# A transformer layer on one core: VectorE's order in the prologue, the first step's tables of units, and the place of the last Tanh

## What is computed

```python
qkv = einsum('bse,fe->bsf', layernorm(x), in_proj_weight) + in_proj_bias
scores = where(blocked, -inf, einsum('bhqd,bhkd->bhqk', q * scale, k))
x = x + einsum('bse,fe->bsf', softmax(scores) @ v, out_proj_weight) + out_proj_bias
h = layernorm(x) @ weight @ aux_weight1 @ aux_weight2
x = x + tanh(h + bias)
```

## Time and profile before

| | us |
|---|---|
| median of 3 runs | 1992.54 |
| lowest and highest | 1991.99 and 1997.41 |
| the profiled execution's own time | 1995.04 |
| its span | 1993.3 |
| ACT busy in it | 1911.1 (96%) |
| PE busy in it | 1819.7 (91%) |
| DVE, POOL busy in it | 1005.1, 440.7 |

### The profile page before, as it was taken

How to read it: one execution, slowest core, us unless ns; L and a number is a source line. 1 busy time by engine, 2 the same in 40 slices (tenths; PEclk the granted TensorE clock), 3 DMA queues, 4 the chain that set the end, 5 groups by cost and what they waited for, 6 DMA issues and landing times.

```text
span 1993.3 us, 101806 instructions
## 1 busy us (share of the span) xinstructions
PE 1819.7 (91%) x47112; PEld 750.0 (38%) x47112; DVE 1005.1 (50%) x1723; ACT 1911.1 (96%) x2099; POOL 440.7 (22%) x458
## 2 busy tenths in 40 slices
PE   6899999999999999999999999999998889888895
PEld 3443343343434434343343434334343323223232
DVE  5333346556474564747556474655635333342432
ACT  4699999999999999999999999999999999999993
POOL 2000004132050412305141130504113210313001
PEclk9999999999999999999999999999999999999998
DMA  4410111101221111111212111111022111000001
GB/s 135 119 51 25 46 33 49 41 28 40 80 76 47 44 38 33 49 36 54 59 53 69 38 51 36 49 49 33 19 78 56 33 32 30 27 22 29 25 25 45
DMA packets 95523, 93.89 MB, mean 47 GB/s; under 512 B 19626, under 2 KB 86634, under 8 KB 95090
## 3 DMA queue, kind: packets, MB, share of 16 engines
q1 hardware_dynamic: 94580, 86.86, 14.8%
q10 hardware_dynamic: 512, 0.47, 0.1%
HBM read 52.56 MB, written 25.72 MB: 39 GB/s over the span
## 4 chain that ended last, share of the span: by engine, by line
ACT 60%; issue 31%; PE 6%; DVE 1%; DMA 1%; POOL 0%; ACTq 0%; SPq 0%; DVEq 0%; POOLq 0%
ACT probs L1362 60%; PE outs L1431 2%; PE scores L1410 1%; PE ps_qk L510 1%; PE spare L1459 0%; PE scores L1628 0%; PE spare L1518 0%; DVE xn L382 0%; DMA inverse<-row_inverse 0%; DVE stats L371 0%; PE ps_turn L483 0%; POOL rstd L314 0%; DMA xin<-in_x 0%; PE spare L1446 0%; PE scores L1646 0%
## 5 line engine op out<-in xcount | busy, mean ns | idle before, releaser
L1362 ACT ACTIVATE probs<-scores 128x1024 f32<-128x1024 f32 x2048 | 1881.1, 1113 | 20.4 <-PE scores L1410 19.9
L1431 PE MATMUL outs<-probs,vs 64*32 64x512 f32 x16384 | 1073.9, 590 | 0.9 <-ACT probs L1362 0.6
L1410 PE MATMUL scores<-qs,ks 49*32 49x512 f16 x16384 | 834.6, 382 | 130.5 <-ACT probs L1362 127.1
L1410 PEld LDWEIGHTS scores<-qs,ks 49*32 49x32 f16 x16384 | 231.6, 89 | 1055.1 <-ACT probs L1362 1032.1
L1431 PEld LDWEIGHTS outs<-probs,vs 64*32 64x32 f32 x16384 | 301.0, 106 | 27.8 <-issue 5.5
L967 DVE TENSOR_TENSOR probs<-probs,allowed 128x320 f32<-128x320 f32 (+2 forms) x280 | 157.0, 564 | 213.6 <-ACT probs L1362 212.1
L875 POOL TENSOR_TENSOR s_squares<-s_qk_f 128x512 bf16<-128x512 f32 x48 | 61.6, 1282 | 293.7 <-DVE s_qk_f L1037 293.7
L1470 PE MATMUL spare<-s_xt,w_qkv 64*32 64x256 f32 x3072 | 119.4, 376 | 0.0
L975 DVE COPY raw<-outs 128x512 f32<-128x512 f32 x32 | 22.1, 692 | 168.0 <-PE outs L1431 119.6
L919 POOL TENSOR_TENSOR t_over<-t_over,t_square 128x512 f32<-128x512 f32 x70 | 94.7, 1353 | 5.8
L861 POOL TENSOR_TENSOR s_var_eps<-s_mean_var,eps 128x4 f32<-128x4 f32 x12 | 2.4, 201 | 414.4 <-DVE s_mean_var L1008 414.4
(11 more groups left out here) (151 smaller groups left out, 1379.1 us busy)
## 6 DMA issues: line engine op xcount, KB each, us to landing
qs<-q_parts SPq DMA_DIRECT2D x192, 64.0 KB
ks<-k_parts SPq DMA_DIRECT2D x189, 64.0 KB
inverse<-row_inverse SPq DMA_DIRECT2D x32, 256.0 KB
shared<-in_x SPq DMA_DIRECT2D x64, 128.0 KB, 2.3
out<-s_pre SPq DMA_DIRECT2D x64, 128.0 KB, 1.9
ctx_in<-raw SPq DMA_DIRECT2D x248, 32.0 KB
s_xin<-in_x SPq DMA_DIRECT2D x48, 128.0 KB, 2.1
q_parts<-s_parts SPq DMA_DIRECT2D x24, 256.0 KB, 2.4
```

The source lines that it names most:

```text
L1362: act.activation(probs[:, u % RING, 2 * slot:2 * slot + 2].rearrange("p c q -> p (c q)"), scores[:, 2 * slot:2 * slot + 2].rearrange("p c ...
L1410: last = pe.matmul(scores[cols, 2 * slot + e], ks[rows, group, keys], qs[rows, group], start=True, stop=True)
L1431: last = pe.matmul(outs[32 * c:32 * c + 32, side], vs[keys, at:at + 2 * HD], probs[keys, u % RING, c], start=(i == 0), stop=(i == KBLOCKS ...
```

## The change

It has four parts.

1. **Prologue.** The first chunk of x comes as two DMAs of two tiles each, and VectorE's third bn_stats waits for the second. `xn_done` is raised for each tile of the first chunk, and TensorE transposes tile by tile (both halves of a tile, then the next). GpSimd's memset of `guard_row` waits for the four tiles and no longer for `rstd` alone. VectorE's order of a chunk becomes: normalise the next chunk first, two splits, `take_norms`, statistics of the chunk after next, two splits.
2. **First step.** Statistics and normalising of step 0 move from r = 0, 1, 5, 6 to r = 8, 9, 13, 14.
3. **Fold.** Each product becomes four pieces of `product` behind units 56 to 59 and 61, 62, 63, 66 (unit 66 is r = 2 of step 1), its sums in two PSUM banks; VectorE takes it with a copy and an add (`take_fold`) at units 60 and 67.
4. **Last Tanh.** It stands behind ScalarE's last Exp, and its addition on VectorE behind the last unit, ahead of `evacuate`.

```diff
-FOLD_AT = (56, 60)
+FOLD_AT = ((56, 57, 58, 59), (61, 62, 63, 66))
+NORMALISE_AT = (0, 1, 5, 6)
+FIRST_NORMALISE_AT = (8, 9, 13, 14)
-SQUASH_AT = {True: 73, False: 58}
...
-            sp.dma_start(xin[:, 0], x_tiles[0]).then_inc(x_in[0], 16)
+            sp.dma_start(xin[:, 0, 0:2], x_tiles[0][:, 0:2]).then_inc(x_in[0], 16)
+            sp.dma_start(xin[:, 0, 2:4], x_tiles[0][:, 2:4]).then_inc(x_rest_in, 16)
...
-            pool.wait_ge(rstd_done, 1)
+            pool.wait_ge(xn_done, TPC)
             pool.memset(guard_row[:], GUARD_K).then_inc(cleared, 1)
...
             def step(c):
                 par = c % 2
+                if c < CPB - 1:
+                    normalise_b(c + 1)
                 dve.wait_ge(parts_out[par], c // 2 * 64)
-                more = c < CPB - 1
-                if more:
-                    normalise_a(c + 1)
                 split(c, 0)
-                if more:
-                    normalise_b(c + 1)
                 split(c, 1)
                 if c:
                     take_norms(c - 1)
+                if c < CPB - 2:
+                    normalise_a(c + 2)
                 for j in range(2, 4):
                     split(c, j)
...
             normalise_b(0)
+            normalise_a(1)
...
-            pe.wait_ge(xn_done, 1)
-            turn(0, 0)
-            turn(0, 1)
+            for t in range(TPC):
+                pe.wait_ge(xn_done, t + 1)
+                for half in range(HALVES):
+                    first = pe.transpose(ps_turn[half][:, t * P:(t + 1) * P], xn[:, t, half * P:(half + 1) * P], ident[:])
+                    if t == TPC - 1:
+                        first.then_inc(turned, 1)
...
+            def take_fold(stage):
+                dve.wait_ge((a12_ready, ffn_ready)[stage], 1)
+                folded = (a12, keep["w_ffn"][:])[stage]
+                dve.tensor_copy(folded, spare[0][:].rearrange("p (h n) -> p h n", n=EMB)).then_inc(dve_step, 1)
+                dve.wait_ge(dve_step, next(dve_steps))
+                dve.tensor_tensor(folded, folded, spare[1][:].rearrange("p (h n) -> p h n", n=EMB), ALU.add
+                                  ).then_inc((a12_copied, ffn_copied)[stage], 1)
...
-                        if c == TAIL - 1 and at == SQUASH_AT[beside] + 2:
-                            add_squashed(c)
...
+            add_squashed(TAIL - 1)
             evacuate(f, 1)
...
-                for c, at, beside in finishing(step, r):
-                    if c == TAIL - 1 and at == SQUASH_AT[beside]:
-                        squash(c)
+            squash(TAIL - 1)
```

More of the change, by code:

```diff
@@ L370, in normalise_a @@
                 for t in range(TPC):
+                    if c == 0 and t == 2:
+                        dve.wait_ge(x_rest_in, 16)
                     dve.bn_stats(stats[:, t], xin[:, c, t]).then_inc(stats_step, 1)
@@ L383, in normalise_b @@
                                              ALU.subtract, ALU.mult)
-                last.then_inc(xn_done, 1)
+                    if c == 0:
+                        last.then_inc(xn_done, 1)
+                if c:
+                    last.then_inc(xn_done, 1)
             def split(c, j):
@@ L1257, in run_step @@
                             write_guard(step // CPB)
-                    if step == 0 and r == FOLD_AT[0] + 2:
-                        dve.wait_ge(a12_ready, 1)
-                        dve.tensor_copy(a12, spare[0][:].rearrange("p (h n) -> p h n", n=EMB)).then_inc(a12_copied, 1)
-                    if step == 0 and r == FOLD_AT[1] + 2:
-                        dve.wait_ge(ffn_ready, 1)
-                        dve.tensor_copy(keep["w_ffn"][:], spare[1][:].rearrange("p (h n) -> p h n", n=EMB)
-                                        ).then_inc(ffn_copied, 1)
+                    for stage in range(2):
+                        if step * STEP + r == FOLD_AT[stage][-1] + 1:
+                            take_fold(stage)
                     if finishes:
@@ L1433, in weigh @@
                 last.then_inc(summed, 1)
-            def fold_ffn(stage):
-                if stage == 0:
-                    pe.wait_ge(ffn_in, 3 * 16)
-                    pe.wait_ge(v_copied, (LATE + 1) * 2)
-                else:
-                    pe.wait_ge(a12_copied, 1)
-                left, right, done = ((a1t, a2s, a12_ready), (w1t, a12, ffn_ready))[stage]
-                for half in range(HALVES):
-                    for k in range(HALVES):
-                        last = pe.matmul(spare[stage][:, half * EMB:(half + 1) * EMB],
-                                         left[:, k, half * P:(half + 1) * P], right[:, k],
-                                         start=(k == 0), stop=(k == HALVES - 1))
-                last.then_inc(done, 1)
             def turned_tiles(tiles, pair, k):
@@ L1472, in product, with fold_ffn @@
                 return last
+            def fold_ffn(stage, i):
+                half, k = divmod(i, HALVES)
+                if i == 0:
+                    if stage == 0:
+                        pe.wait_ge(ffn_in, 3 * 16)
+                        pe.wait_ge(v_copied, (LATE + 1) * 2)
+                    else:
+                        pe.wait_ge(a12_copied, 1)
+                left, right, done = ((a1t, a2s, a12_ready), (w1t, a12, ffn_ready))[stage]
+                last = product(half * EMB, lambda rows, c: left[rows, k, half * P + 32 * c:half * P + 32 * c + 32],
+                               right[:, k], k)
+                if i == 3:
+                    last.then_inc(done, 1)
             def turn(step, i):
@@ L1607, in run_step @@
                             sum_squares(step)
-                    if step == 0 and r in FOLD_AT:
-                        fold_ffn(FOLD_AT.index(r))
+                    for stage in range(2):
+                        if u in FOLD_AT[stage]:
+                            fold_ffn(stage, FOLD_AT[stage].index(u))
                     for pair in range(2):
```

12 lines of the change are left out of this document (7 added, 5 removed).

## The result

| | before | after |
|---|---|---|
| median of the runs of this comparison, us | 1994.38 (4 runs) | 1979.57 (4 runs, 1977.76 to 1980.35) |
| ratio, 95% interval | | 0.9925 (0.9911 to 0.9939) |
| span of the profiled execution, us | 1993.3 | 1976.0 |

The change takes 14.8 us off, against 13.1 forecast. A later comparison of the same two kernels gives 13.4 (1992.81 to 1979.38); the nine runs of the changed kernel have the median 1979.38.

What follows compares the result with a forecast made beforehand. ScalarE's chain of 2048 Exps was taken to set the pace from 65.61 us on. Gains of 6.0 + 5.2 + 2.2 - 0.3 = 13.1 us take the median from 1992.54 to 1979.4, 8 in 10 within 1977 to 1984.

Steps and rivals of the forecast that it cites:

- Prologue: Everything ahead of ScalarE's first Exp: it starts earlier, a gain of 6.0 us (4.5 to 6.7).
- Start: First chunk of the prologue: first projection at 11.4 against 14.31, a gain of 2.9 us (2.3 to 3.3).
- the landing of the second half of x: First chunk's second DMA: lands between 4.7 and 5.3 us, taken as 4.95.
- The step from the transposes to the projection: First chunk: 0.78 us as before plus 0.5 because the two copies stand behind each other.
- Order: VectorE in chunks 2 and 3: chunk 2's transposes 4.5 us earlier, 1.6 beyond the start; chunk 3 gains 1.4 to 2.1 more.
- SP's queue: End of the prologue: SP, free at 49.65 for a split done at 49.1, cuts off the end of the gain.
- Memset: First chunk's normalising: 3.27 us while GpSimd's memset ran, 1.39 for the same four tiles elsewhere; the memset now waits.
- First step: Start of the stream: ScalarE's 5.5 us of waits go, 0.3 put for TensorE's own work; gain 5.2 (4.5 to 5.5).
- The rival that another link holds it: Units 3 to 6 of the first step: another link keeps half of the 5.5 us; time 1982, chance 0.13.
- Fold: Where the fold runs: two ScalarE waits of 2.3 us go, eight pieces are covered; gain 2.2 us (-1.7 to 2.3).
- Last Tanh: End of the stream: addition and four stores ahead of the sums; loses 0.3 us (gain 0.4 to loss 0.9).
- The rival of a lasting fall: TensorE's clock falls to 1.2 GHz from units 0 to 3 and stays, 1.7 us lost per unit; chance 0.03.

Runs made afterwards that it cites:

- p_memset: Changed kernel with GpSimd's memset of guard_row waiting for the reciprocal root alone again; normalising to first projection 5.1 us against 3.6, single run 1978.89 us.
- u_tanh: Changed kernel with part 4 undone (Tanh behind unit 58 of the last step, its addition two units later); 1978.73 us, ratio 0.9921 to the kernel before.
- v_tail: Changed kernel with the last Tanh's addition behind evacuate and SP's four stores behind the moves of sums and inverse; 1978.34 us, ratio 0.9924 to the kernel before.
- v_store: Changed kernel with the last Tanh's addition behind evacuate and SP's four stores behind the scaling of the context; 1977.89 us, ratio 0.9915 to the kernel before.
- v_best: Changed kernel with v_store's two tail edits and v_warm's idle-time matmuls in three places together; 1983.12 us, ratio 0.9946 to the kernel before.
- v_warm: Changed kernel with unread idle-time TensorE work in three places (22 transposes, 18 transposes, 24 matmuls); 1981.26 us, ratio 0.9940 to the kernel before.
- after_again: The changed kernel word for word, run again in the third comparison; 1979.38 us, ratio 0.9929 to the kernel before.
- p_turn: Changed kernel with TensorE waiting for all four tiles of the first chunk before transposing; 4.25 us from normalising to first projection, against 3.64.

## Why the prediction was right, point by point

- **Total.** 13.1 forecast; 14.8 by the first comparison, 13.4 by the later one. The forecast's own likeliest band (1978 to 1981) holds the 1979.57.
- **Prologue, 6.0 forecast (4.5 to 6.7), 7.2 in the trace and 7.4 by undoing it.** The mechanism was right, the size short, in part by the luck of this profile: 7.2 is against a first Exp at 58.37, and against the 58.89 in the middle of the seven it is 6.7. *Start:* 3.6 and not 2.9. The term that failed is the landing of the second half of x. I put it at 4.95, nearer the whole's 4.74; in 9 of the 12 profiles with the split it landed at 4.2 to 4.4, when VectorE wanted it or 0.1 later, and in three it held VectorE up until 4.80 to 5.45. The step from the transposes to the projection (0.78 + 0.5) was 1.14. *Order:* half 1 of chunk 2's transposes 5.8 earlier and not 4.5. Those are 3.6 of the start, 0.6 because the first twelve projections took 7.16 us and not 7.76 (they scatter up to 8.45, so that is luck), and 1.6 of the order, just as forecast: from the end of ScalarE's group (1,1) to the transposes it is 1.84 us (25.78 to 27.62) and was 3.45 (29.96 to 33.41). Chunk 3's come 7.8 earlier where the working gave 5.9 to 6.6; the period is 9.49, at the short end of 9.4 to 10.1. *SP's queue:* I let it cut off the end. It issued the third store at 48.25, 0.6 behind its split, but was free at 48.76, ahead of the end of the last split at 49.00, so it cost nothing; that step of the prediction was wrong. What did take some back is the landing of the last k part, 3.15 us and not the 2.35 of before, of which the load of the guards behind it (2.95 for 3.21) gave 0.3 back, and so 7.8 became 7.2 at the first Exp. *Memset:* the 1.9 us that I put down to the one memset were two, 1.5 of `guard_row` and 0.4 of `vs` (p_memset); the gain is of both, since both now stand behind the four tiles.
- **First step, 5.2 forecast.** 4.8 by the waits of the kernel without it, and 0.40 us is left within the first units where 0.3 was put for it. The rival that another link holds it falls.
- **Fold, 2.2 forecast.** 2.24 by the two waits that come back. The eight pieces are covered, as the sixteen of the same form were. VectorE's two copies and two adds show nowhere.
- **Last Tanh, a loss of 0.3 forecast (gain 0.4 to loss 0.9).** Loss of 0.6 to 1.0 up to the sums' arrival, against u_tanh. Two steps held: the addition was held up beside GpSimd's (1.51 to 1.81 us in the nine profiles of this form, 1.57 in after, and 1.21 or 1.22 where it stands behind `evacuate`), and the four stores stand ahead of the sums. The Trainium skill (SBUF — State Buffer, section Who interferes with whom) says that a VectorE instruction with two SBUF inputs contends with a GpSimd instruction that reads SBUF; the row of 1.57 against 1.21 agrees with it. The tile of 1.86 us in p_memset is not that case: it has one tile as its input, and the memset beside it only writes. `evacuate` began 1.53 us behind ScalarE's end where I had 1.83; the sums' landing took 2.88 to 3.27 us in eight profiles (2.45 or 2.46 in u_tanh, v_tail, v_store and v_best, with no stores issued right ahead of them), an extra that I had bounded at 0 to 0.6 and left at 0 in the sum. That the stores cause it is not shown: it took 2.40 in v_warm, with the four stores as close ahead, and 2.82 in the kernel before.
- **Clock.** The rival of a lasting fall didn't come, but a short one did. It moved with the start:

```profile
57.90:59.00 1.10, 1.10 (x56) 0.86 0.09 30
59.00:62.00 3.00, 3.00 (x104) 0.50 0.17 49
62.00:64.00 2.00, 1.07 (x56) 0.98 0.25 69
```

These are windows of TensorE in after (the granted clock stands behind the count in brackets). It had waited 2.77 us for the first score. Before, the fall stood at 75 to 80 us, behind 3.47 us in which TensorE waited for the late values, which are now gone. The 0.40 us wait left at 62.76 goes with the new fall: in the profile of after_again, the same kernel, the clock reads 1.00 in every us from 58 to 65 and the first 18 Exps run without a gap, while u_tanh, v_tail, v_store, p_turn and p_memset fall to 0.50 or near it between 59 and 64 and show 0.2 to 0.8 us waits there.

- **The 17.3 us between the two spans** are 7.2 (first Exp) + 5.1 (first step) + 2.3 (fold) - 0.2 (up to the sums' issue), 14.4 in all, and 2.9 that I can't trace to a part of the change: ScalarE's other scattered waits were 2.7 us before and 1.9 after; its pitch over 1884 us gives 0.8; and from the issue of the sums to the end before took 31.25 us and after 29.98, since the inverse landed 0.4 sooner and TensorE's clock came back earlier in the output projections (5.52 us for sixteen against 6.53; the profiles without added work scatter from 5.50 to 6.68).

## What to carry to other kernels

Where one engine's chain sets the pace for 95% of the time, look at its waits by stretch and at its first start: four local edits there gave what undoing each took away (7.4 + 6.0 + 3.2 - 0.65 = 16 by the medians, against 14.8 and 13.4, which is within what they can tell). Moving work behind the last instruction of the bounding engine is no gain if it puts another engine's instruction and another queue's transfers ahead of the tail's first transfer: write that first transfer's path free, then place the rest. And price a filler by a row of its own form, counting instructions as the trace does.

## What the runs showed of the hardware that I had not expected

- The first f32 projections of the program run at half pace (0.88 us for one instruction of 128x512 against 0.41) behind TensorE's idle start, and not where 22 transposes ran ahead of them with a gap of 0.72 us; with a gap of 1.83 us, 1.4 us of the slowness was back. The granted clock reads 1.00 over it in the kernels without the added work and 0.50 in the last one, so a reading of 1.00 at the start of a program is no evidence.
- A VectorE instruction that starts 0.08 us behind the start of a GpSimd memset of 1.79 us ends only 0.15 us behind the memset's end: 1.86 us for a tile of 0.41. The second and third tile take 0.40, and the fourth, met by another memset of 0.55 us after it has begun, takes 0.85 (p_memset; the kernel before shows the same 1.86).
- Of two DMAs of 256 KB, issued 0.5 us apart, the first lands 1.0 to 1.2 us ahead of one of 512 KB. The second lands at 4.2 to 4.4, some 0.4 ahead of it, in 9 of 12 profiles, and in three of them not until 4.80 to 5.45, later than the one did (4.74 and 4.79).
